# Gated cross-attention and ternary FFN on one core: plain V products for the second context too, an earlier read-out on ScalarE, and moved ternary steps

## The chip, the cores and the metric

The kernel runs on one core of a Trainium2 chip. Times are device microseconds (us) of that core. The kernel before took 1602.74 us, the median of 3 runs (1601.34 to 1603.58). Engines are named as in the profile: PE is TensorE's matmul, PEld its weight load, DVE is VectorE, ACT is ScalarE, POOL is GpSimd, SP is SyncE, which issues most DMAs.

## The reference

For 8 batches of 1024 rows and 512 channels, with g0 and g1 two gates:

```
q, k, v = layernorm(x) @ w_q, ctx @ w_k, ctx @ w_v
s       = (q @ k.T) / sqrt(512), causal mask
x       = x + tanh(g0) * (softmax(s) @ v)
h       = gelu(layernorm(x) @ ternary(W1).T + b1)        # W1: 2048 x 512
out     = x + tanh(g1) * (h @ ternary(W2).T + b2)        # W2: 512 x 2048
ternary(w) = clip(round(w / mean|w|), -1, 1)
```

All of it is computed near float32: an operand is held as a high and a low float16 half, and a product is three passes (`PASSES`: high·high, low·high, high·low). The ternary weights are exact in float16 and need two passes.

## The kernel before

**Two phases.** The attention runs over 64 slots. Slot t works on row tile t (128 rows); eight tiles (`TB`) share one batch, so tile i = t mod 8 of a batch sees i + 1 blocks of its context. Behind the slots the FFN runs over 16 groups of 4 tiles, in 64 units (`NU`).

**One slot on PE.** Scores of tile t (`s_ps`, 12 matmuls per 512 columns), the product that makes the query side of tile t + 2 (`t_product`, 24 matmuls of 256 columns), a part of the V projection of the next batch, then softmax times V of tile t - 1 (`o_ps`). The scores' width grows with i, so slots with i = 0 or 1 are short and those with i = 7 long. Scores of an even slot wait for `t_lower` (DVE) of the odd slot before it (`t_split`).

**V in two ways.** The first batch's V is made tile by tile: `v_product`, 12 matmuls of 512 columns each, read out by `v_upper` (ACT) and `v_lower` (DVE). From the second batch on a pair of tiles (256 rows) is a 2 x 2 block matrix, and a seven-product scheme makes it: products 1 to 7 of 6 matmuls of 256 columns (`v_part`). There are `NP` = 28 pairs. Pair u starts in slot 4 + 2u (`SPLIT_AT`: sums of the context's blocks on POOL, `ctx_parts`), has products 1 and 2 at the end of the odd slot 5 + 2u (`PRE_AT`, `v_pre`), products 6, 5, 7, 3 in the even slot 6 + 2u (`MAIN_AT`) and product 4 in slot 7 + 2u (`LAST_AT`). Products 1, 6, 5 and 3 share one PSUM bank `vp_a`; so product 6, the first thing that PE does in an even slot, waits until ACT has copied product 1 to `vr` (`v_first`, `vr_out`), and product 5 until ACT has copied product 6 (`v_second`, L737), which itself waits for `v21_lower` (DVE, L1104) of the pair before. The sums of weight blocks for it are split in `weight_parts_upper` (ACT, slot 4) and `weight_parts_lower` (DVE, slots 4 and 5, L1053).

**Order.** The program is written out by hand: each engine has a `slot` function that calls the pieces in its own order, and each engine runs them strictly in that order; semaphores join them. In an odd slot ACT does `softmax`, `t_upper` (L785), `rows_upper` (L793, which waits for DVE's `ln_rows`, L1133), and only then `v_first` (L730) and `v21_upper` (L761). DVE does mask and maximum (L1193, L1195), layernorm statistics, `p_split` (L1215), `t_lower` (L1156), `ln_rows`, the V read-outs, a ternary step where there is one, and then the update of `x_ring` with the attention's output (L1259), for which PE waits one tile later.

**Ternary weights.** 16 chunks of 1024 columns are made ternary by three DVE instructions each (`ternary`, L1393 to L1396), 12 of them in slots set by the "T" entries of `W_PLAN`, 4 in the first units of the FFN. **First FFN rows.** In slots 57 to 62 the first tiles' second layernorm is already made (`y_stats`, `y_normal`, and on POOL `y_scale`, `y_sums`, `y_lower`); `add_bias` (POOL, L640) adds b2 to the residual of the first four tiles in slots 61 and 62. `weight_sums` (DVE, L1298, slots 61 and 62) makes sums of W1 blocks.

## Time and profile before

| what | value |
|---|---|
| median of 3 runs | 1602.74 us |
| the profiled execution's own time | 1603.13 us |
| its span | 1601.3 us |
| PE busy | 1560.5 us (97%) |
| DVE busy | 1173.0 us (73%) |
| ACT busy | 881.7 us (55%) |
| POOL busy | 608.6 us (38%) |
| mean DMA rate | 107 GB/s |

A span is from the first to the last instruction; the time is the span and what lies around it, here 1.8 us. PE's busy time is read as time in which matmuls were in flight; it isn't work at full rate, since at the half clock the same matmul takes twice as long. The idle time of an engine counts only where the next engine in the chain waits for it.

### The profile page before, as it was taken

Reading aid. Unit: us, or ns where it says so; the run is one execution under the profiler, and the core shown is the slowest. Engines: PE = TensorE matmul, PEld = TensorE weight load, DVE = VectorE, ACT = ScalarE, POOL = GpSimd, SP = SyncE. Lnnn points to the kernel's source line nnn. Section 1 sums busy time; section 2 is a strip of 40 time slices with the busy share of each in tenths; the row PEclk is TensorE's granted clock in tenths of the full one; section 3 lists DMA queues with packets and bytes.
Section 4 is the critical chain, followed back from the end, with each engine's and each line's share of the span. In section 5 each row is a group of like instructions: output and inputs, shape, how many; then the busy total and the mean of one; then the engine's idle time right before and its main releaser. Section 6 shows DMA issues by size and latency. Waiting matters only on the chain.

```text
span 1601.3 us, 27829 instructions
## 1 busy us (share of the span) xinstructions
PE 1560.5 (97%) x10528; PEld 1028.5 (64%) x10528; DVE 1173.0 (73%) x1993; ACT 881.7 (55%) x1595; POOL 608.6 (38%) x585
## 2 busy tenths in 40 slices
PE   8889999999999999999999999999999999999998
PEld 4556666666666666665666666666666666666665
DVE  5767868788888888877776676767776677667654
ACT  4334545544444444344666666666666666666664
POOL 4323323332333323344353453444344443345320
PEclk9999999999999999999999999999999999999999
DMA  7536767756455545545523242223223333224110
GB/s 210 139 88 149 175 146 186 158 132 147 117 147 138 150 113 148 124 120 114 142 76 74 54 99 76 76 47 99 77 77 65 81 85 85 78 51 100 50 50 27
DMA packets 310997, 170.92 MB, mean 107 GB/s; under 512 B 268544, under 2 KB 268560, under 8 KB 310608
## 3 DMA queue, kind: packets, MB, share of 16 engines
q1 hardware_dynamic: 309392, 166.52, 43.1%
q10 hardware_dynamic: 1296, 2.36, 0.4%
q8 instruction: 83, 1.36, 0.3%
q14 instruction: 50, 0.41, 0.1%
q0 software_dynamic: 176, 0.27, 0.1%
HBM read 70.53 MB, written 33.55 MB: 65 GB/s over the span
## 4 chain that ended last, share of the span: by engine, by line
PE 74%; DVE 16%; issue 4%; ACT 4%; DMA 1%; SPq 0%; POOL 0%; DVEq 0%; ACTq 0%
PE s_ps L1556 13%; PE e_ps L1556 13%; PE s_ps L1692 7%; PE t_ps L1498 7%; PE o_ps L1498 7%; PE v_ps L1498 7%; PE o_ps L1739 6%; PE t_ps L1651 5%; PE e_ps L1594 4%; PE m_ps L1498 3%; DVE ctx_s L982 2%; DVE negmax L1195 1%; DVE x_ring L1259 1%; DVE xn_both L1133 1%; DVE v_work L1061 1%
## 5 line engine op out<-in xcount | busy, mean ns | idle before, releaser
L1350 DVE SCALAR_TENSOR_TENSOR v_s<-xnT,sc,v_s 128x512 f16<-128x512 f32 x256 | 238.6, 952 | 106.2 <-ACT v_s L909 106.2
L902 ACT ACTIVATE xnT<-tT,b_s 128x256 f32<-128x256 f32 x384 | 174.0, 500 | 179.7 <-DVE tT L1338 64.9
L1556 PE MATMUL s_ps<-raw,v_s 128*128 128x512 f16 x1024 | 263.0, 380 | 0.8 <-DVE raw L1396 0.8
L1556 PE MATMUL e_ps<-raw,v_s 128*128 128x512 f16 x1024 | 262.9, 379 | 0.0
L1692 PE MATMUL s_ps<-ctx_s,tT 128*128 128x512 f16 (+3 forms) x1152 | 202.0, 331 | 3.4 <-DVE tT L1156 2.6
L1739 PE MATMUL o_ps<-v_s,pT 128*128 128x512 f16 x840 | 193.2, 382 | 2.4 <-DVE x_ring L1259 2.4
L909 ACT ACTIVATE v_s<-xnT,sc 128x512 f16<-128x512 f32 x256 | 176.2, 712 | 7.5
L1556 PEld LDWEIGHTS e_ps<-raw,v_s 128*128 128x128 f16 x1024 | 100.2, 98 | 120.8
L646 POOL TENSOR_TENSOR tT<-tT 128x512 f32<-128x512 f32 x64 | 81.2, 1269 | 244.5 <-ACT tT L929 244.5
L1651 PE MATMUL t_ps<-xnT,a_s 128*128 128x256 f16 x1488 | 172.8, 273 | 0.1
L559 POOL TENSOR_TENSOR rstd<-var_s,minus_half 128x1 f32<-128x1 f32 x61 | 59.9, 983 | 291.8 <-DVE var_s L1127 291.8
L1692 PEld LDWEIGHTS s_ps<-ctx_s,tT 128*128 128x128 f16 x1152 | 107.1, 99 | 93.0 <-issue 6.2
L1651 PEld LDWEIGHTS t_ps<-xnT,a_s 128*128 128x128 f16 x1488 | 145.4, 98 | 20.9 <-DMA xnT<-xn_both 0.3
L1556 PEld LDWEIGHTS s_ps<-raw,v_s 128*128 128x128 f16 x1024 | 100.1, 98 | 68.1 <-issue 1.1
L1739 PEld LDWEIGHTS o_ps<-v_s,pT 128*128 128x128 f16 x840 | 82.5, 98 | 90.7 <-issue 4.9
L770 ACT ACTIVATE p<-s_ps,ebias,esc 128x128 f32<-128x128 f32 (+3 forms) x64 | 53.1, 830 | 154.3 <-DVE ebias L1199 154.0
L563 POOL TENSOR_TENSOR xn_both<-xn_both 128x512 f16<-128x512 f32 x61 | 70.5, 1156 | 151.3 <-ACT xn_both L793 151.3
L614 POOL TENSOR_TENSOR rstd<-var_s,minus_half 128x1 f32<-128x1 f32 x64 | 36.2, 565 | 221.8 <-DVE var_s L1310 221.8
L1332 DVE COPY tT<-t_ps 128x512 f32<-128x512 f32 x64 | 44.2, 691 | 85.0 <-PE t_ps L1498 85.0
L793 ACT ACTIVATE xn_both<-xn_both 128x512 f16<-128x512 f32 x64 | 40.3, 629 | 100.3 <-DVE xn_both L1133 100.3
L1594 PE MATMUL e_ps<-v_work 128*128 128x256 f16 x504 | 70.7, 278 | 20.7 <-ACT vr L730 16.3
L1344 DVE TENSOR_TENSOR tT<-tT,t_ps 128x512 f32<-128x512 f32 x64 | 44.0, 688 | 50.3 <-ACT tT L923 26.2
(229 smaller groups left out, 2882.7 us busy)
## 6 DMA issues: line engine op xcount, KB each, us to landing
out_y<-x_ring SPq DMA_DIRECT2D x128, 256.0 KB, 2.2
x_ring<-in_x SPq DMA_DIRECT2D x63, 256.0 KB, 2.9
raw<-in_ctxT SPq DMA_DIRECT2D x28, 512.0 KB, 3.8
v_work<-out_y SPq DMA_DIRECT2D x40, 256.0 KB, 3.8
w_in<-in_w1T SPq DMA_DIRECT2D x16, 512.0 KB, 3.9
w_in<-in_w2T SPq DMA_DIRECT2D x12, 512.0 KB, 4.0
x_ring<-out_y SPq DMA_DIRECT2D x22, 256.0 KB, 4.0
xnT<-xn_both SPq DMA_TRANSPOSE x128, 2.5
```

Of the source, the lines that this page charges most:

```text
L559: g.tensor_tensor(rstd[:, r:r + 1], var_s[:, r:r + 1], minus_half[:, :], ALU.pow).then_inc(ln_rstd, 1)
L563: g.tensor_tensor(xn_s[:, r, LO], xn32[:, r], xn_s[:, r, HI], ALU.subtract).then_inc(xn_lo, 1)
L646: g.tensor_tensor(rr[:, R3], rr[:, R3], rr[:, R5], ALU.add).then_inc(c22_sum, 1)
L902: a.activation(g32n[:, j, half * 2 * P:(half + 1) * 2 * P], src, ACT.Gelu, bias=b1_s[:, f:f + 1], scale=1.0 / YN).then_inc(g_act, 1)
L909: a.activation(g_s[:, U % 2, j, HI], g32n[:, j], ACT.Copy, scale=col(C_SG)).then_inc(g_hi, 1)
L1350: v.scalar_tensor_tensor(out=g_s[:, U % 2, j, LO], in0=g32n[:, j], scalar=col(C_SG), in1=g_s[:, U % 2, j, HI], op0=ALU.mult, op1=ALU.subtr ...
L1498: last_mm = mm(bank[:, p * 2 * P:(p + 1) * 2 * P], w, yT[g % 2][:, a, row, c, :], start=(first and p == 0 and a == HI and c == 0), stop=(a ...
L1556: last_mm = mm(y_ps[i], g_s[:, U % 2, j, a, i * P:(i + 1) * P], w2_s[:, f, :], start=(U % UG == 0 and n == 0 and a == HI), stop=(U % UG == ...
L1594: last_mm = mm(bank, left(ca, c), right(va, c), start=(first and n == 0 and c == 0), stop=(n == 2 and c == 1), skip_group_check=True)
L1651: last_mm = mm(bank[:, dd], a_s[:, aa, c, d * P:(d + 1) * P], xnT[:, pr, xa, c, :], start=(n == 0 and c == 0), stop=(n == 2 and c == DC - 1))
L1692: last_mm = mm(s_ps[:, lo:hi], tT[:, pr, ta, c, q * P:(q + 1) * P], ctx_s[:, par, ca, c, lo:hi], start=(n == 0 and c == 0), stop=(n == 2 a ...
L1739: last_mm = mm(o_bank(last, s), pT[:, (s - 1) % 2, pa, j], v_s[:, par, va, j], start=(n == 0 and j == 0), stop=(n == 2 and j == jn))
```

## The change

`PLAIN` = 2 batches now have their V made tile by tile. `v_product`, `v_upper` and `v_lower` run while t + 1 < 16 instead of t + 1 < 8, so 8 tiles move to the plain way and `NP` falls from 28 to 24 pairs; the four numbers `SPLIT_AT` to `LAST_AT` become 12 to 15. The second context is scaled and split in slots 5, 6 and 7 (`FIRST_SPLITS`), the third is loaded one slot behind each. Its maxima are taken in slots 8, 10 and 11. `weight_parts_lower` moves from slots 4 and 5 to 5 and 6. `v_first` moves on ACT ahead of `rows_upper`, for every pair but the first. The ternary steps of slots 31, 39 and 56 go to 32, 40 and 60; the buffers of the last ones change, and the waits for `x2_biased` and `w_ternary` with them. The four first `add_bias` go behind the slots, to POOL's start of the FFN.

```
-        NP = (NT - TB) // 2
-        SPLIT_AT, PRE_AT, MAIN_AT, LAST_AT = 4, 5, 6, 7
+        PLAIN = 2
+        NP = (NT - PLAIN * TB) // 2
+        SPLIT_AT, PRE_AT, MAIN_AT, LAST_AT = (TB * (PLAIN - 1) + n for n in (4, 5, 6, 7))
+        FIRST_SPLITS = {5: (0,), 6: (1, 2), 7: (3,)}
...
-                  **{t: "T" for t in (29, 30, 31, 37, 38, 39, 45, 46, 53, 54, 55, 56)}}
+                  **{t: "T" for t in (29, 30, 32, 37, 38, 40, 45, 46, 53, 54, 55, 60)}}
...
-                    sp.wait_ge(w_ternary, NW - W_LATE)
+                    sp.wait_ge(w_ternary, NW - W_LATE - 1)
...
+                for q in FIRST_SPLITS.get(t - 1, ()):
+                    load_ctx(2, q)
...
-                if last and e in (4, 5):
-                    add_bias(2 * e - 8)
-                    add_bias(2 * e - 7)
...
             last_sum(0)
             y_lower(2)
+            for e in range(GT):
+                add_bias(e)
...
                     t_upper(it, s)
+                if pre is not None and pre:
+                    v_first(pre)
                 if not last or t + LN_LEAD < NT:
                     rows_upper(it, s)
                 if t == 1:
                     ctx_upper(0, 0, 3)
+                for q in FIRST_SPLITS.get(t, ()):
+                    ctx_upper(1, 1, q)
                 if t == 4:
                     weight_parts_upper()
-                if t + 1 < TB:
+                if t + 1 < PLAIN * TB:
                     v_upper(it, s)
-                if pre is not None:
+                if pre == 0:
                     v_first(pre)
...
-                if t in (4, 5):
-                    weight_parts_lower(t - 4)
-                if t + 1 < TB:
+                if t in (5, 6):
+                    weight_parts_lower(t - 5)
+                if t + 1 < PLAIN * TB:
                     v_lower(it, s)
...
-                if n == NW - W_LATE:
-                    dve.wait_ge(x2_biased, 2)
...
-                v.tensor_scalar(w_neg[:, :], src, col(nth), None, ALU.is_lt).then_inc(w_negs, 1)
+                neg = w_neg[:, :]
+                if n == NW - W_LATE - 1:
+                    neg = w_in[:, (m + 1) % WR].bitcast(F16)[:, 0:WCH]
+                if n >= NW - W_LATE:
+                    neg = pT[:, 0, 0].rearrange("p j n -> p (j n)")
+                v.tensor_scalar(neg, src, col(nth), None, ALU.is_lt).then_inc(w_negs, 1)
...
-                if t + 1 < TB and t != PRE_AT:
+                if t + 1 < PLAIN * TB and t != PRE_AT:
                     v_product(it, s)
```

PE from the scores of slot 7 on, before: `t_ps` is the query product, the rows with `v_work` or a width of 256 in `e_ps` and `v_ps` are parts of the seven products, `o_ps` is softmax times V.

```order
L1692 MATMUL s_ps<-ctx_s,tT 128x512 x24
L1651 MATMUL t_ps<-xnT,a_s 128x256 x24
L1594 MATMUL e_ps<-v_work,ctx_s 128x256 x6
L1594 MATMUL e_ps<-wv_s,ctx_s 128x256 x6
L1594 MATMUL v_ps<-wv_s,ctx_s 128x256 x6
L1739 MATMUL o_ps<-v_s,pT 128x512 x21
L1594 MATMUL e_ps<-v_work 128x256 x6
L1692 MATMUL s_ps<-ctx_s,tT 128x128 x12
```

The same place now; L1682 is the plain product.

```order
L1704 MATMUL s_ps<-ctx_s,tT 128x512 x24
L1663 MATMUL t_ps<-xnT,a_s 128x256 x24
L1682 MATMUL v_ps<-wv_s,ctx_s 128x512 x12
L1751 MATMUL o_ps<-v_s,pT 128x512 x21
L1704 MATMUL s_ps<-ctx_s,tT 128x128 x12
```

All pieces of the seven products are gone from slots 5 to 13, and one plain product stands in each.

ACT in slot 33, an odd slot with i = 1, before: the first row is the exponential, then the high half of p, `t_upper`, `rows_upper` (L793), `v_first` (L730), `v21_upper` (L761) and, of the next slot, `v_second` (L737) and `v_third`.

```order
L770 ACTIVATE p,rowsum<-s_ps,ebias,esc 128x256
L775 ACTIVATE p_s<-p 128x256
L785 ACTIVATE tT<-t_ps 128x512
L793 ACTIVATE xn_both<-xn_both 128x512
L730 ACTIVATE vr<-e_ps 128x256
L761 ACTIVATE v_s<-vr 128x256
L737 ACTIVATE vr<-e_ps 128x256
L742 ACTIVATE vr<-e_ps 128x256
```

And now, with `v_first` as L733 and `rows_upper` as L796.

```order
L773 ACTIVATE p,rowsum<-s_ps,ebias,esc 128x256
L778 ACTIVATE p_s<-p 128x256
L788 ACTIVATE tT<-t_ps 128x512
L733 ACTIVATE vr<-e_ps 128x256
L796 ACTIVATE xn_both<-xn_both 128x512
L764 ACTIVATE v_s<-vr 128x256
L740 ACTIVATE vr<-e_ps 128x256
L745 ACTIVATE vr<-e_ps 128x256
```

Only the fourth and fifth row change places: `v_first` no longer stands behind an instruction that waits for DVE's `ln_rows`.

DVE in slot 60 from `t_lower` on, before: three V read-outs, the update of `x_ring` (L1252 to L1259), `y_normal` (L1324), and the mask of slot 61.

```order
L1156 SCALAR_TENSOR_TENSOR tT<-t_ps,tT 128x512
L1076 TENSOR_TENSOR vr<-vr,e_ps 128x256
L1088 SCALAR_TENSOR_TENSOR v_s<-e_ps,v_s 128x256
L1096 SCALAR_TENSOR_TENSOR v_s<-vr,v_s 128x2x256
L1252 RECIPROCAL rinv<-rowsum 128x1
L1255 TENSOR_SCALAR osc<-rinv,fsc 128x1
L1259 SCALAR_TENSOR_TENSOR x_ring<-o_ps,osc,x_ring 128x512
L1324 TENSOR_SCALAR v_s<-x_ring,mv,rstd 128x512
L1193 TENSOR_TENSOR s_ps<-s_ps,causal 128x128
```

And now.

```order
L1163 SCALAR_TENSOR_TENSOR tT<-t_ps,tT 128x512
L1083 TENSOR_TENSOR vr<-vr,e_ps 128x256
L1095 SCALAR_TENSOR_TENSOR v_s<-e_ps,v_s 128x256
L1103 SCALAR_TENSOR_TENSOR v_s<-vr,v_s 128x2x256
L1405 TENSOR_SCALAR w_in<-w_in,sc 128x1024
L1406 TENSOR_SCALAR raw<-w_in,sc 128x1024
L1408 TENSOR_TENSOR raw<-raw,w_in 128x1024
L1259 RECIPROCAL rinv<-rowsum 128x1
L1262 TENSOR_SCALAR osc<-rinv,fsc 128x1
L1266 SCALAR_TENSOR_TENSOR x_ring<-o_ps,osc,x_ring 128x512
L1333 TENSOR_SCALAR v_s<-x_ring,mv,rstd 128x512
L1200 TENSOR_TENSOR s_ps<-s_ps,causal 128x128
```

The ternary step that stood in slot 56 now stands ahead of the update of `x_ring` in slot 60.

## Rows read from the trace of the kernel before

**Rows 1.** The page: span, busy time of PE, the chain's shares by engine.
```profile
span 1601.3 us, 27829 instructions
...
PE 1560.5 (97%) x10528; PEld 1028.5 (64%) x10528; DVE 1173.0 (73%) x1993; ACT 881.7 (55%) x1595; POOL 608.6 (38%) x585
...
PE 74%; DVE 16%; issue 4%; ACT 4%; DMA 1%; SPq 0%; POOL 0%; DVEq 0%; ACTq 0%
```

**Rows 2.** Waits of PE, 60 to 770 us: us in total, times, longest.
```profile
PE e_ps L1594 <- ACT vr L730: 16.3, 13, 3.2
PE e_ps L1594 <- DVE v_work L1053: 4.3, 1, 4.3
PE o_ps L1739 <- DVE x_ring L1259: 2.4, 1, 2.4
```

**Rows 3.** Stretches: length, busy by engine (x instructions), then PE's clock, DMA.
```profile
102.71:109.54 6.83, 5.42 (x16) 2.34 (x17) 4.03 (x6) 0.38 (x1) 3.26 (x4) 0.50 0.34 86
423.57:426.98 3.41, 3.41 (x14) 1.79 (x13) 3.16 (x6) 0.44 (x2) 3.33 (x5) 0.50 0.32 92
```

**Rows 4.** Timeline of PE, slots 4 and 8: start, us, instruction, [idle before].
```profile
80.83 2.75 PE L1670 MATMUL v_ps<-wv_s,ctx_s 128*128 128x512 f16 x12
83.42 0.38 PE L1739 MATMUL o_ps<-v_s,pT 128*128 128x512 f16 x1
...
141.92 0.82 PE L1594 MATMUL e_ps<-v_work 128*128 128x256 f16 x6
142.58 0.82 PE L1594 MATMUL e_ps<-wv_s,v_work 128*128 128x256 f16 x6
```

**Rows 5.** Timeline of DVE and PE where slot 6 begins.
```profile
102.18 1.79 DVE L1053 SCALAR_TENSOR_TENSOR v_work<-v_s,sc,v_work 128x1024 f16<-128x1024 f32 x1
...
104.12 1.44 PE L1594 MATMUL e_ps<-v_work 128*128 128x256 f16 x6 [4.29 <-DVE v_work L1053]
```

**Rows 6.** Timeline of DVE, ACT and PE at the end of slot 9.
```profile
154.01 0.69 DVE L1156 SCALAR_TENSOR_TENSOR tT<-t_ps,tT 128x512 f16<-128x512 f32 x1
155.18 0.63 ACT L793 ACTIVATE xn_both<-xn_both 128x512 f16<-128x512 f32 x1 [2.00 <-DVE xn_both L1133]
155.72 0.36 ACT L730 ACTIVATE vr<-e_ps 128x256 f32<-128x256 f32 x1
156.14 0.83 PE L1594 MATMUL e_ps<-v_work 128*128 128x256 f16 x6 [1.02 <-ACT vr L730]
156.52 0.81 DVE L1104 SCALAR_TENSOR_TENSOR v_s<-vr,v_s 128x256 f16<-128x256 f32 x1
```

**Rows 7.** Timeline of PE where slots 34 and 58 begin.
```profile
423.38 1.31 PE L1594 MATMUL e_ps<-v_work 128*128 128x256 f16 x6 [2.24 <-ACT vr L730]
...
693.31 1.46 PE L1594 MATMUL e_ps<-v_work 128*128 128x256 f16 x6 [3.18 <-ACT vr L730]
```

**Rows 8.** The ternary lines in the slots: ns min/median/max; one POOL bias add.
```profile
L1393 DVE TENSOR_SCALAR g<-w_in,sc x12: 740/1209/1271, 377.0 to 682.4; 128x1024 f16<-128x1024 f32 x12
L1394 DVE TENSOR_SCALAR w_s<-w_in,sc x8: 740/1210/1214, 378.2 to 571.7; 128x1024 f16<-128x1024 f32 x8
L1396 DVE TENSOR_TENSOR w_s<-w_s,g x8: 693/1095/1098, 379.4 to 572.5; 128x1024 f16<-128x1024 f16 x8
740.96 1.26 POOL L640 TENSOR_TENSOR v_work<-g,b_row 128x512 f32<-128x512 f32 x1
```

**Rows 9.** Timeline, slots 56 to 61: PE's scores of 57, then DVE.
```profile
683.42 1.47 PE L1692 MATMUL s_ps<-ctx_s,tT 128*128 128x256 f16 x12
684.87 0.75 DVE L1259 SCALAR_TENSOR_TENSOR x_ring<-o_ps,osc,x_ring 128x512 f32<-128x512 f32 x1
693.36 0.42 DVE L1070 TENSOR_TENSOR vr<-vr,v_ps 128x256 f32<-128x256 f32 x1 [0.71 <-ACT vr L730]
697.74 0.30 DVE L1193 TENSOR_TENSOR s_ps<-s_ps,causal 128x128 f32<-128x128 f32 x1 [1.17 <-PE s_ps L1692]
740.24 0.75 DVE L1259 SCALAR_TENSOR_TENSOR x_ring<-o_ps,osc,x_ring 128x512 f32<-128x512 f32 x1
```

More of the change, by code:

```diff
@@ L237, in pair_at @@
         def pair_at(u):
-            b, q = 1 + u // NQ, u % NQ
+            b, q = PLAIN + u // NQ, u % NQ
             return b, q, b % 2
@@ L247, in gated_block @@
         B12_DONE, BD_DONE, B21_DONE = 1, 2, 3
-        MAX_AT = {2: (1, (0, 1)), 3: (1, (2, 3))}
-        for b in range(2, B):
+        MAX_AT = {2: (1, (0, 1)), 3: (1, (2, 3)), 8: (2, (0, 1)), 10: (2, (2,)), 11: (2, (3,))}
+        for b in range(PLAIN + 1, B):
             for q, at in enumerate((-3, -1, 1, 3)):
@@ L268, in gated_block @@
         W_CHUNKS = [(src, dst, k) for src, dst in ((w1T, w1_s), (w2T, w2_s)) for k in range(DC * FC * P // WCH)]
-        W_FIRST = NQ * 6
+        W_FIRST = NQ * (B - 1 - PLAIN)
         NW = len(W_CHUNKS)
@@ L365, in load_ctx @@
                 sp.wait_ge(ctx_split, NQ * (batch - 1) + q + 1)
-                if batch >= 2:
-                    sp.wait_ge(sums_made, 4 * (NQ * (batch - 2) + q + 1))
+                if batch > PLAIN:
+                    sp.wait_ge(sums_made, 4 * (NQ * (batch - 1 - PLAIN) + q + 1))
                 sp.dma_start(raw_q[:, q], ctx_batches[batch][:, q]).then_inc(ctx_in[q], 16)
@@ L451, in slot @@
                 if u is not None and u + NQ < NP:
-                    load_ctx(2 + u // NQ, u % NQ)
+                    load_ctx(PLAIN + 1 + u // NQ, u % NQ)
                 if last and t == NT - 8:
@@ L1262, in slot @@
                     ctx_lower(0, 0, 3)
+                for q in FIRST_SPLITS.get(t, ()):
+                    ctx_lower(1, 1, q)
                 if t in MAX_AT:
@@ L1598, in v_pre @@
             def v_pre(u):
-                pe.wait_ge(ctx_split, NQ + u + 1)
+                pe.wait_ge(ctx_split, NQ * PLAIN + u + 1)
                 if u:
@@ L1604, in v_pre @@
                 if u == 1:
-                    pe.wait_ge(v_split, TB)
+                    pe.wait_ge(v_split, PLAIN * TB)
                 if u:
@@ L1725, in slot @@
                     pe.wait_ge(p_turned[(s - 1) % 2], p_turned_by(it, s - 1))
-                    if t <= TB:
+                    if t <= PLAIN * TB:
                         pe.wait_ge(v_split, t)
                     else:
-                        u = (t - 1 - TB) // 2
+                        u = (t - 1 - PLAIN * TB) // 2
                         pe.wait_ge(vb_split, nth_of(u, B12_DONE))
```

2 lines of the change are left out of this document (1 added, 1 removed).

## The prediction, made before the changed kernel had run

> **What bounds the kernel now.** I read the page first: PE is busy for 1560.5 of 1601.3 us, and the chain that ended last lies on PE for 74% and on DVE for 16% [rows 1]. So a microsecond is won only where PE does less, stops standing, or stops running at half clock. The second view is PE's waits over the slots [rows 2]: three groups matter. Thirteen times product 6 of a pair waits for ScalarE's read-out of product 1 (16.3 us in total); once it waits for DVE's weight sums (4.3); once the product with V waits for DVE's update of `x_ring` (2.4). The third view is the granted clock by stretch [rows 3]: behind the wait of 4.3 us PE runs 6.83 us at 0.50, its lower level of 1.2 GHz, and behind the wait of 2.24 us in slot 33 it does so for 3.41 us. Work done at that level would have taken half the time at 2.4 GHz, so the first stretch costs 5.42 / 2 = 2.7 us and the second 3.41 / 2 = 1.7. The timelines then say what the waiting instruction really waited for. The FFN behind the slots is PE without a gap to speak of, and the change leaves its products as they are.
>
> **Plain instead of seven products (slots 5 to 15).** A plain product starts at 80.83 and the next work at 83.42, so it is 2.59 us of PE; six matmuls of 256 columns go from 141.92 to 142.58, 0.66 us [rows 4]. A pair costs 7 x 0.66 = 4.6 us in seven products and 2 x 2.59 = 5.2 plain, so four pairs add 4 x 0.6 = +2.4 us. This is work on PE, and nothing hides it.
>
> A rule in the Trainium skill would have it otherwise (TensorE: Matmul & The Clock Gate, "Back-to-back issue gap"): it gives 131 ns per matmul of 512 columns in a sustained stream and 81 ns at 128. By it a plain product would be 12 x 131 ns = 1.6 us and, with 106 ns between the two for 256 columns as an estimate, the pair would save about 1.3 us, 5 us for four. By that rule the sum would come out 7 us lower. The trace does not agree: it has 216 ns for each of these very matmuls [rows 4]. The measurement decides, and I give the rule no chance.
>
> What it takes away: product 6 in slot 6 waited 4.29 us for the second `weight_parts_lower`, which ended at 103.97 because it stands in DVE's queue behind a wait for `v_first` [rows 5]. Now these sums are made in slots 5 and 6 and first used in slot 14, eight slots later, so wait and half clock go: -4.3 - 2.7 = -7.0 us. What is late next in slot 13, where the first pair's product 1 is read out in the old place? There ScalarE's queue holds `rows_upper` and `v_upper` ahead, as in slot 5; but DVE comes to the mask without the weight sums of 1.3 to 1.8 us and without their wait for ScalarE, and PE has a product with V of 15 matmuls (15 x 0.216 = 3.2 us) before it asks. I take no wait, and keep up to 1.5 us in the range. In the plain slots DVE has one read-out of a bank per slot instead of six smaller instructions and the low half of the sums per pair, so it gets lighter; the scaling of the second context comes to slots 5 to 7, which are long on PE (i = 5 to 7). The third context's four loads are issued by SP at the end of slots 6 to 8 and used by DVE at the end of slots 8 to 11, a slot or more later; what stands behind them on SP are the transposes of rows used two slots later. I take 0 for both.
>
> **`v_first` ahead of `rows_upper`.** In slot 9 [rows 6] ScalarE stood 2.00 us for DVE's `ln_rows`, then did `rows_upper` (0.63) and only at 155.72 the read-out, which PE had been waiting for since 155.12 (156.14 - 1.02). Product 1 ends before product 2 and the product with V, so in the new place the read-out falls into those 2.00 us: it costs ScalarE nothing, and it is done before PE is. What is late next? Product 6 then starts at 155.12 and the scores of slot 10 at 155.78; they need `t_lower`, which ended at 154.70: 1.1 us to spare. Product 5 comes 12 x 0.162 = 1.9 us later (384 columns), at 157.7; it needs the read-out of product 6, which stands behind `v21_lower`, ended at 157.33 before and some 0.4 us earlier now, because ScalarE no longer has 0.36 us of `v_first` ahead of `v21_upper`. So 157.0 + 0.4 = 157.4: just in time. In slots with i = 3 the scores are wider and there is more room. The thirteen waits are those of the slots with i = 1 and 3, two of which fall into slots 9 and 11, where now there are no seven products at all. I take twelve of them whole: 16.3 - 3.2 (slot 57, below) = -13.1 us. In slot 33 the wait was 2.24 us and was followed by half clock [rows 3, 7]: a further -1.7 us.
>
> **Ternary steps.** A step is 3.5 us where POOL works beside it and 2.1 us where it doesn't (medians 1.21 + 1.21 + 1.10, least 0.74 + 0.74 + 0.69 [rows 8]). POOL makes the context's block sums at the start of even slots, which is when DVE gets to the step of slot 31 or 39; in slots 32 and 40 the step comes when POOL has only the norm, and just ahead of an update of `x_ring` that waits for PE anyway. So DVE comes to slots 33 and 41 no later than now, rather about a microsecond earlier, and this is what lets me take the 2.24 us whole.
>
> The Trainium skill (SBUF — State Buffer, "SBUF: two separate sides") says that DVE in a two-port mode and GpSimd take one shared pair of ports as an exclusive lock. The trace has both prices for the same instruction, 0.74 and 1.21 us, so it agrees as far as it goes; if slot 60's step met such work after all, the sum would be 1.4 us higher.
>
> Slot 57 is different. Its wait of 3.18 us [rows 7] with the half clock behind it (1.7) ought to be worth 4.9 us, and PE does come to slot 58 that much earlier. But from there DVE is the engine that is behind: from the update at 684.87 to the one at 740.24 [rows 9] it rarely stands, and PE waits for the last one (2.4 us [rows 2]). So this stretch is worth what DVE's path becomes. Without the step in slot 56 the update can start about where the product that it reads ends and PE's next scores start, 683.42; with 0.3 us for the end of that product, 683.7: -1.2. The wait for `v_first` goes: -0.7. The wait for PE's scores goes, since PE is early: -1.2. The step now in slot 60, with POOL at rest: +2.1. Sum -1.0 us instead of -4.9. PE's wait in slot 61 becomes longer, about 3.5 to 4 us, partly moved to the scores of slot 62; the half clock behind it may grow by up to 1 us.
>
> **First residual sums.** Four adds of 1.26 us each [rows 8] leave POOL in slots 61 and 62, where they ran beside `y_normal` and beside the last p split on DVE; this may give some tenths at the last product with V. In the FFN they stand behind `y_lower` and ahead of `y_scale` of a group that isn't urgent; their sums are asked for only when the first group is finished, some units later. I take 0, at worst 4 x 1.26 = 5 us of delay for `y_scale` and, with the first units full of PE work, none of it on the path.
>
> **Sum.** +2.4 - 7.0 - 13.1 - 1.7 - 1.0 = -20.4 us against the profiled execution's 1603.13, so 1582.7. That execution was 0.4 us above the median shown, so against the median 1582.3; I say 1582.
>
> **Rivals.**
> 1. *The waits of product 6 come back at the next place*: at the scores (`t_lower`) or at product 5 (`v_second`), because DVE, which had a rest of 0.7 us in each of these waits, is now driven faster than it can go in the short slots. For it: only some 0.3 us to spare at product 5 by my own working. Against: scores had 1.1 us to spare. Ten waits remain outside slots 9, 11 and 57, 11.3 us (13.1 less 1.9); half of it back is +5.7, all but the clock +8: 1588 to 1590.
> 2. *Slot 57's gain is kept*: -4.9 instead of -1.0, and no longer half clock: 1578. Against it is the row of the wait at slot 61; for it, that DVE's waits inside the stretch (for ACT and for POOL's `y_lower`) may shrink too.
> 3. *Slower*: `v_first` now holds ScalarE's queue until PE has finished product 1, and behind it stand `rows_upper`, POOL's low half, SP's transposes and the query product. The place is every odd slot from 15 on, 23 of them. If rows then came late, each would cost PE what ScalarE is late; it decides from 20.4 / 23 = 0.9 us a slot; at 1 us it costs 23. Against: product 1 is done before `ln_rows` in rows 6, and the rows are used two slots later. It would give 1582.7 + 23 = 1606.
> 4. *The change doesn't do what it says in slots 4 to 15*: a wait in slot 13 or in the plain slots like the 4.29 us, with its clock loss: +7, 1589.
>
> **Chances.** Forecast 0.68 (its own range 1580 to 1585), rival 1 0.12, rival 2 0.10, rival 3 0.03, rival 4 0.07. The unknowns within the forecast (1.5 us in slot 13, 1.4 us for the step in slot 60, 1 us of clock, some tenths at the end) and the runs' spread of 2.2 us give 1580 to 1586; to leave out no more than 2 in 10 I take in rival 2 and most of rivals 1 and 4, 1577 to 1589. A change under 0.2% (3.2 us) can't be told from none: faster 0.95, same 0.02, slower 0.03.
>
> **What would show it.** Right: no row of PE waiting for the read-out of product 1 but perhaps in slot 13; no granted clock of 0.50 near 103 and near 424; the plain products in slots 4 to 14 at 2.59 us without gaps; seven-product matmuls down from 1176 to 1008; a longer wait of PE for `x_ring` in slot 61, at a time about 20 us earlier than 741; the FFN as long as before. Wrong: waits of PE for `t_lower` or the second read-out of a microsecond each in slots with i = 1, or PE's wait in slot 61 gone.

## The result, and the profile after

The changed kernel takes 1586.12 us (median of 4 runs, 1584.63 to 1586.78), the kernel before, run beside it, 1603.16 (1601.34 to 1604.01). The ratio is 0.9894, with a 95% interval of 0.9877 to 0.9911: 17.0 us faster. 20.4 us and 1582 were forecast, so the change gives a sixth less than that; the time lies inside the range given (1577 to 1589), but outside the forecast's own (1580 to 1585).

The page of the changed kernel, which answers to [rows 1]: the span, the busy times, the chain.

```profile
span 1582.8 us, 27584 instructions
...
PE 1554.9 (98%) x10456; PEld 1019.6 (64%) x10456; DVE 1165.2 (74%) x1973; ACT 871.8 (55%) x1575; POOL 590.3 (37%) x569
...
PE 72%; DVE 16%; ACT 5%; issue 4%; DMA 1%; POOL 0%; SPq 0%; DVEq 0%; ACTq 0%
```

PE is still the bound. It is busy for only 5.6 us less than before, while the span fell by 18.5: most of the gain is time in which PE stood. PE's waits over 60 to 790 us say which standing went, and what came (beside [rows 2]; the line numbers are those of the changed kernel, L1606 a seven-product matmul, L740 the read-out of product 6, `v_second`, L1266 the update of `x_ring`, L1163 `t_lower`, L1341 the FFN's first copy on DVE):

```profile
PE e_ps L1606 <- ACT vr L740: 4.0, 6, 1.3
PE o_ps L1751 <- DVE x_ring L1266: 3.5, 1, 3.5
PE s_ps L1704 <- DVE tT L1163: 1.9, 3, 0.7
PE t_ps L1510 <- DVE tT L1341: 1.4, 1, 1.4
PE e_ps L1751 <- DMA pT<-p_s: 0.4, 1, 0.4
```

No row is left of PE waiting for product 1's read-out (16.3 us before) or for the weight sums (4.3). Two rows are new: six waits for the *other* read-out, 4.0 us, and one of 1.4 us at the start of the FFN. Granted clock by stretch, against [rows 3] (the third column from the end is PE's clock):

```profile
32.63:36.05 3.42, 3.42 (x18) 2.43 (x17) 3.35 (x5) 2.04 (x2) 2.26 (x1) 0.50 0.01 2
101.00:108.00 7.00, 7.00 (x48) 4.43 (x46) 4.75 (x11) 2.65 (x5) 0.55 (x1) 1.00 0.39 95
412.00:419.00 7.00, 6.82 (x55) 5.11 (x53) 6.41 (x15) 2.74 (x7) 3.70 (x6) 1.00 0.55 135
722.13:725.54 3.41, 3.41 (x10) 1.20 (x9) 2.30 (x6) 1.91 (x3) 0.55 (x1) 0.50 1.00 213
```

Near 103 us and in slots 33 and 34 PE now has 2.4 GHz, and the stretch of half clock that followed the wait of 3.18 us in slot 57 is gone too; behind the wait of 3.5 us it still falls to 1.2 GHz, as it did before. The first row is worth a look, because it isn't the change's doing: of the kernel before the same place reads

```profile
31.03:37.86 6.83, 4.84 (x23) 3.46 (x24) 6.52 (x14) 2.38 (x4) 3.89 (x2) 0.50 0.20 49
```

The start is the same program in both. Of the profiled executions of this study some had the short stretch there and some the long one (the experiments e7 and f2, for instance, the long one). The profiled execution of the changed kernel is its fastest run of four and has the short one. Slot 5's scores, which start 1.2 us earlier in it than in the kernel before, lie between 84.0 and 85.2 us in the seven profiled executions with the short stretch and between 85.4 and 86.7 in the seven with the long one. So spans are compared from a fixed instruction behind the start, slot 4's scores, and whole times by their medians.

The span by stretch, from PE's rows of both kernels at the same places: scores of slots 5, 16 and 57, and the FFN's first product with W2. Before:

```profile
86.01 4.06 PE L1692 MATMUL s_ps<-ctx_s,tT 128*128 128x512 f16 x24
226.64 0.83 PE L1692 MATMUL s_ps<-ctx_s,tT 128*128 128x128 f16 x12
...
771.29 1.03 PE L1556 MATMUL s_ps<-raw,v_s 128*128 128x512 f16 x4
```

After:

```profile
84.80 4.06 PE L1704 MATMUL s_ps<-ctx_s,tT 128*128 128x512 f16 x24
218.27 0.83 PE L1704 MATMUL s_ps<-ctx_s,tT 128*128 128x128 f16 x12
...
664.87 1.47 PE L1704 MATMUL s_ps<-ctx_s,tT 128*128 128x256 f16 x12
...
751.47 1.03 PE L1568 MATMUL s_ps<-raw,v_s 128*128 128x512 f16 x4
```

With 683.42 of [rows 9] for slot 57 before, the lengths are:

| stretch | before | after | difference | forecast |
|---|---|---|---|---|
| start to slot 5 | 86.01 | 84.80 | -1.2 | 0 |
| slots 5 to 16 (plain V) | 140.63 | 133.47 | -7.2 | +2.4 - 7.0 - 1.9 = -6.5 |
| slots 16 to 57 | 456.78 | 446.60 | -10.2 | -11.2 - 1.7 = -12.9 |
| slot 57 to the FFN's first product | 87.87 | 86.60 | -1.3 | -1.0 |
| the rest | 830.01 | 831.33 | +1.3 | 0 |
| span | 1601.3 | 1582.8 | -18.5 | -20.4 |

Without the 1.2 us at the start, it is 17.3, about what the medians say. Set against the forecast that leaves some 3 us missing, in two places: slots 16 to 57 (2.7), and the start of the FFN (1.3); slots 5 to 16 and the end of the slots gave 1.0 more.

### The profile page after: what moved, and what is told of

Read it like the earlier page. It is cut to its first block, busy times and chain, and to the rows that moved or that the text cites. A ratio compares the mean times of both kernels' runs of the same rounds, so it can differ in the third digit from the quotient of the medians.

```text
span 1582.8 us, 27584 instructions
## 1 busy us (share of the span) xinstructions
PE 1554.9 (98%) x10456; PEld 1019.6 (64%) x10456; DVE 1165.2 (74%) x1973; ACT 871.8 (55%) x1575; POOL 590.3 (37%) x569
## 4 chain that ended last, share of the span: by engine, by line
PE 72%; DVE 16%; ACT 5%; issue 4%; DMA 1%; POOL 0%; SPq 0%; DVEq 0%; ACTq 0%
PE s_ps L1568 14%; PE e_ps L1568 13%; PE t_ps L1510 7%; PE v_ps L1510 7%; PE o_ps L1510 7%; PE o_ps L1751 6%; PE s_ps L1704 5%; PE t_ps L1663 5%; PE m_ps L1510 3%; PE e_ps L1606 2%; PE v_ps L1682 2%; DVE negmax L1202 2%; DVE ctx_s L989 2%; DVE x_ring L1266 1%; DVE xn_both L1140 1%
## 5 line engine op out<-in xcount | busy, mean ns | idle before, releaser
L1359 DVE SCALAR_TENSOR_TENSOR v_s<-xnT,sc,v_s 128x512 f16<-128x512 f32 x256 | 239.5, 956 | 105.7 <-ACT v_s L916 105.7
L1704 PE MATMUL s_ps<-ctx_s,tT 128*128 128x512 f16 (+3 forms) x1152 | 197.7, 326 | 4.7 <-DVE tT L1163 3.9
L563 POOL TENSOR_TENSOR rstd<-var_s,minus_half 128x1 f32<-128x1 f32 x61 | 56.0, 919 | 291.7 <-DVE var_s L1134 291.7
L615 POOL TENSOR_TENSOR rstd<-var_s,minus_half 128x1 f32<-128x1 f32 x64 | 36.1, 565 | 218.8 <-DVE var_s L1319 218.8
L1341 DVE COPY tT<-t_ps 128x512 f32<-128x512 f32 x64 | 44.2, 691 | 85.0 <-PE t_ps L1510 85.0
L796 ACT ACTIVATE xn_both<-xn_both 128x512 f16<-128x512 f32 x64 | 40.3, 630 | 90.5 <-DVE xn_both L1140 90.0
L641 POOL TENSOR_TENSOR v_work<-v_work,b_row 128x512 f32<-128x512 f32 x40 | 75.4, 1913 | 0.0
```

Source lines behind the costliest of these rows:

```text
L563: g.tensor_tensor(rstd[:, r:r + 1], var_s[:, r:r + 1], minus_half[:, :], ALU.pow).then_inc(ln_rstd, 1)
L641: g.tensor_tensor(x2, x2_first(e), b2_row[:, :], ALU.add).then_inc(x2_biased, 1)
L1359: v.scalar_tensor_tensor(out=g_s[:, U % 2, j, LO], in0=g32n[:, j], scalar=col(C_SG), in1=g_s[:, U % 2, j, HI], op0=ALU.mult, op1=ALU.subtr ...
L1704: last_mm = mm(s_ps[:, lo:hi], tT[:, pr, ta, c, q * P:(q + 1) * P], ctx_s[:, par, ca, c, lo:hi], start=(n == 0 and c == 0), stop=(n == 2 a ...
```

## The experiments

Each time stands beside the kernel before on the same chip; "gain" is the difference of these medians, and the changed kernel's is 17.0. A gain's interval is 2 to 3 us to each side, so smaller differences between two experiments are read from their traces. "From slot 4 on" is the time from the start of slot 4's scores to the end of the profiled execution; a table behind the last experiment has it for every run.

### One part at a time: the read-out, the plain context

e1 undoes only the place of `v_first` in the changed kernel:

```
-                if pre is not None and pre:
-                    v_first(pre)
                 if not last or t + LN_LEAD < NT:
                     rows_upper(it, s)
...
-                if pre == 0:
+                if pre is not None:
                     v_first(pre)
```

> The changed kernel (1586.1 us) with one thing undone: the read-out of product 1 stands behind rows_upper again in every odd slot. My theory (the read-out's place is worth the waits of product 6 in slots 15 to 55): the waits for that read-out come back in the slots with i = 1 and 3, ten or eleven of 0.7 to 1.3 us and the one of slot 57, 11 to 13 us in sum less what DVE gives back at the 3.5 us wait in slot 61; the time is 1595 to 1598. Rival A (the steps moved to slots 32 and 40 and not the read-out's place took the waits away): no more than 3 us, 1587 to 1589. Rival B (the waits only hid DVE's lag, and come out elsewhere): the waits for product 1 come back but those for the second read-out and x_ring go, 1590 to 1592.

Measured: 1591.32 us against 1602.95, ratio 0.9936 (0.9923 to 0.9949), gain 11.6. My number (1595 to 1598) was wrong. Rival B had the time, and half of the account: the waits for the second read-out go, as it says, but that for `x_ring` stays at 3.5 us. PE's waits of e1:

```profile
PE e_ps L1604 <- ACT vr L733: 11.4, 11, 2.0
PE o_ps L1749 <- DVE x_ring L1264: 3.5, 1, 3.5
...
PE s_ps L1702 <- DVE tT L1161: 1.3, 2, 0.7
```

The eleven waits come back whole, 11.4 us, just as counted. But the 4.0 us for the second read-out are gone in exchange, and 0.6 of `t_lower`'s: 11.4 - 4.0 - 0.6 = 6.8, and the two spans, with the same short stretch at the start, are 1589.5 and 1582.8. So the new place removes 11.4 us of waits and earns 6.7 by the traces, 5.4 by the medians.

e2 makes the same move alone, in the kernel before:

```
+                if pre is not None and pre:
+                    v_first(pre)
                 if not last or t + LN_LEAD < NT:
                     rows_upper(it, s)
```

> The kernel before (1603.2 us) with one thing done: the read-out of product 1 ahead of rows_upper for every pair but the first. If the parts add up as in my sum, all thirteen waits of product 6 go but those that a ternary step in slots 31, 39 and 56 causes: 9 to 11 us, the time 1592 to 1594; the wait of 4.3 us near 104 us and its half clock stay. If the new place pays only together with the moved steps, slots 32 and 33, 40 and 41 and 57 still wait, and the waits for t_lower or the second read-out take over elsewhere: 1597 to 1600.

Measured: 1591.28 us against 1602.95, ratio 0.9931 (0.9917 to 0.9945), gain 11.7, a little beyond the first case. The row of its waits for ScalarE:

```profile
PE e_ps L1596 <- ACT vr L737: 5.5, 6, 1.3
```

All thirteen waits for product 1 go, even in slots 33, 41 and 57 with the ternary steps in their old slots, and 5.5 us come for the second read-out. Alone it takes off 11.7; all the rest of the change without it (e1) takes off 11.6; together 17.0 (from slot 4 on 11.0, 10.7 and 17.3). The two don't add up, because both lift the same waits: of the 16.3 us the plain context and the moved steps remove 4.9 anyway, and three of the four stretches of half clock between slot 4 and the end (e1's one stands at 680 us, in slot 58, behind a wait of 2.02 us).

e3 puts the second context back to seven products:

```
-        PLAIN = 2
+        PLAIN = 1
...
-                if t in (5, 6):
-                    weight_parts_lower(t - 5)
+                if t in (4, 5):
+                    weight_parts_lower(t - 4)
```

> The changed kernel with the plain V taken back to the first context alone (28 pairs in seven products, the weight sums in slots 4 and 5, the maxima and splits of the second context as before); the read-out's place, the ternary steps and the residual sums stay as changed. My theory (plain costs 2.4 us and takes away a wait of 4.3 us and 2.7 us of half clock, near 104 us): 1586.1 + 7.0 - 2.4 = 1590.7, between 1589.5 and 1592. Rival A (the second plain context is what saves, waits of its four pairs included): 1593 or more. Rival B (what DVE is late in slot 6 has gone with the read-out's place and steps): no wait near 104, 1583.7.

Measured: 1590.96 us against 1602.95, ratio 0.9929 (0.9916 to 0.9942), gain 12.0: 5.0 less than the changed kernel, where 4.6 was worked out. The wait is back, and with it half clock until 110.5:

```profile
104.82 1.44 PE L1606 MATMUL e_ps<-v_work 128*128 128x256 f16 x6 [4.29 <-DVE v_work L1060]
```

From slot 5's scores to slot 16's e3 takes 138.65 us (86.72 to 225.37), the changed kernel 133.47: 5.2 us.

### The ternary steps

e5 moves two steps back, e6 the last one:

```
-(29, 30, 32, 37, 38, 40, 45, 46, 53, 54, 55, 60)
+(29, 30, 31, 37, 38, 39, 45, 46, 53, 54, 55, 60)      # e5
+(29, 30, 32, 37, 38, 40, 45, 46, 53, 54, 55, 56)      # e6
```

> The changed kernel with two ternary steps back in slots 31 and 39 (from 32 and 40). Theory (with the step ahead of it DVE is late for the mask and the ln_rows of the next slots, and the step costs 3.5 us beside POOL's block sums instead of 2.1): PE waits 1 to 2 us more in slots 32 to 33 and 40 to 41, once perhaps with 1.7 us of half clock behind it: 1588 to 1591. Rival (with the read-out early, slot 33 no longer waits for DVE, so the steps' place is worth nothing): 1585.5 to 1586.5; it could even be shorter, since the waits for the second read-out in slots 32 and 40 (1.3 and 0.7 us) would find DVE at another phase.

Measured: 1586.51 us against 1602.06, ratio 0.9905 (0.989 to 0.992), gain 15.6. My 1588 to 1591 was too high. 1.4 us of 17.0 is less than the intervals can part, but the trace shows where it lies, two slots on and at product 5, not where I looked for it:

```profile
413.31 0.83 PE L1606 MATMUL e_ps<-v_work 128*128 128x256 f16 x6 [0.98 <-ACT vr L740]
501.89 0.83 PE L1606 MATMUL e_ps<-v_work 128*128 128x256 f16 x6 [0.98 <-ACT vr L740]
```

Both waits are 0.18 in the changed kernel. From product 5 of slot 32 to that of slot 34 e5 takes 20.42 us (392.89 to 413.31), the changed kernel 19.27 (393.73 to 413.00): the place of a step is worth 1.15 us, 0.8 of it in this wait, the rest in pauses under 0.2 us. For both that is 2.3 us in the trace and 1.4 in the medians. The step itself takes 3.5 us in slots 31 and 39 of e5 and 2.1 in slots 32 and 40 of the changed kernel, as I had it.

> The changed kernel with the last early ternary step back in slot 56 (from 60). Theory (DVE's path from the update in slot 56 to the last one bounds this stretch): a step of 3.5 us in slot 56 instead of 2.1 us in slot 60, so PE comes to the last product with V 1.2 to 1.5 us later: 1587.3 to 1587.8, and PE waits earlier, in slot 57 or 58, instead of 3.5 us in slot 61. Rival A (PE's waits have gone with the read-out's place, and where the step stands is no matter): 1586. Rival B: the wait in slot 57 is long enough for half clock: 1589.

Measured: 1585.4 us against 1602.06, ratio 0.9895 (0.988 to 0.991), gain 16.7: no difference. The price was wrong: DVE's rows of e6 in slot 56, and its next long wait,

```profile
664.85 0.74 DVE L1405 TENSOR_SCALAR w_in<-w_in,sc 128x1024 f16<-128x1024 f32 x1
665.51 0.74 DVE L1406 TENSOR_SCALAR raw<-w_in,sc 128x1024 f16<-128x1024 f32 x1
666.29 0.69 DVE L1408 TENSOR_TENSOR raw<-raw,w_in 128x1024 f16<-128x1024 f16 x1
...
700.08 0.55 DVE L1333 TENSOR_SCALAR v_s<-x_ring,mv,rstd 128x512 f32<-128x512 f32 x1 [3.79 <-POOL v_s L632]
```

show 2.1 us, as in slot 60, not the 3.5 us beside POOL that I took; it was so in the kernel before too, where the first of them, the last of [rows 8]'s range at 682.4, took 0.74 us. Wherever the step stands, PE waits 5.7 to 5.8 us in slots 56 to 62, only elsewhere: this is DVE's path. And that path holds a wait of 3.79 us for POOL's first `y_lower` (L632).

### What the second read-out waits for

e7 gives product 6's read-out two buffers, so that it doesn't wait for `v21_lower` of the pair before:

```
-        vr = sb("vr", [P, 3, D // 2])
+        vr = sb("vr", [P, 4, D // 2])
...
-                if u:
-                    act.wait_ge(vb_split, nth_of(u - 1, B21_DONE))
-                a.activation(vr[:, 2], vp_a, ACT.Copy).then_inc(vr_out, 1)
+                if u >= 2:
+                    act.wait_ge(vb_split, nth_of(u - 2, B21_DONE))
+                a.activation(vr[:, 2 + u % 2], vp_a, ACT.Copy).then_inc(vr_out, 1)
```

> The changed kernel with two buffers for the read-out of product 6, so that it needn't wait for v21_lower of the pair before. Theory (the six waits for the second read-out, 4.0 us, come from that wait alone; they are the price of my rival 1 in slots with i = 0): they go, and nothing else is late in those slots, 1582 to 1583. Rival (DVE is late as a whole there, and PE waits a moment later for t_lower or the V sums instead): half or less comes out, 1584.5 to 1586.

Measured: 1583.58 us against 1602.06, ratio 0.9882 (0.9866 to 0.9899), gain 18.5, between my two cases; the span is 1581.1, with slot 4's scores at 73.74 (73.09 in the changed kernel), so 2.35 us less from there on. Of the 4.0 us 0.2 are left, and 1.5 come elsewhere, each under 0.6: `t_lower` 0.8 more, product 1's read-out 0.5, a context split 0.2. So the theory holds for the waits that it names, and more than a third of them comes back a moment later, as the rival has it.

Why slots 32, 40 and 48, and not 16 and 24? Rows of the changed kernel at slot 24 and at slot 32 (DVE's `v21_lower`, then PE's product 6; in slot 32 also POOL, the scores, ScalarE's read-out and product 5):

```profile
302.86 1.18 DVE L1111 SCALAR_TENSOR_TENSOR v_s<-vr,v_s 128x256 f16<-128x256 f32 x1 [0.35 <-ACT v_s L764]
304.23 0.82 PE L1606 MATMUL e_ps<-v_work 128*128 128x256 f16 x6
...
390.90 0.82 PE L1606 MATMUL e_ps<-v_work 128*128 128x256 f16 x6
391.56 0.83 PE L1704 MATMUL s_ps<-ctx_s,tT 128*128 128x128 f16 x12
391.76 1.16 POOL L567 TENSOR_TENSOR xn_both<-xn_both 128x512 f16<-128x512 f32 x1 [2.87 <-ACT xn_both L796]
392.02 1.18 DVE L1111 SCALAR_TENSOR_TENSOR v_s<-vr,v_s 128x256 f16<-128x256 f32 x1 [0.34 <-ACT v_s L764]
393.29 0.38 ACT L740 ACTIVATE vr<-e_ps 128x256 f32<-128x256 f32 x1 [1.30 <-DVE v_s L1111]
393.73 0.83 PE L1606 MATMUL e_ps<-v_work 128*128 128x256 f16 x6 [1.34 <-ACT vr L740]
```

In slot 24 `v21_lower` starts 1.4 us ahead of product 6, in slot 32 1.1 us behind it, with two ternary steps on DVE in slots 29 and 30. That these steps make it late is argued and not shown, for no run moves them; and they can't be all of it, since slot 56 has steps in slots 53 to 55 before it, and there `v21_lower` still starts 0.7 us ahead (653.07 and 653.78) and PE doesn't wait. And in a slot with i = 0 the scores between products 6 and 5 are 12 matmuls of 128 columns, 391.56 to 392.39: 0.8 us of cover, where slot 10, on which the forecast was worked, had 1.9.

### The start of the FFN

e4 puts the four residual sums back into slots 61 and 62, e8 puts them behind unit 0:

```
+                if last and e in (4, 5):          # e4
+                    add_bias(2 * e - 8)
+                    add_bias(2 * e - 7)
...
+                if U == 0:                        # e8
+                    for e in range(GT):
+                        add_bias(e)
```

> The changed kernel with the first four residual sums back in slots 61 and 62. Theory (they delay DVE at the start of the FFN, as the new wait of 1.4 us at 768.65 says): that wait goes, y_normal in slot 61 and the last p split are slower again by 0.5 to 1 us; the time is between 1 us shorter and the same, 1585 to 1586. Rival A: the adds in slots 61 and 62 cost DVE as much on the path as they give at the start of the FFN, or more: 1586.5 to 1588.

Measured: 1584.87 us against 1602.95, ratio 0.9891 (0.9877 to 0.9905), gain 18.1.

> The changed kernel with the first four residual sums made by POOL at the end of the FFN's unit 0 instead of ahead of it. Theory (they hold the shared port while DVE makes y_stats and y_normal of slot 62 and the late ternary steps, and that is the new wait of 1.4 us at 768.65): that wait goes, 1584.5 to 1585. Rival A: the contention only moves to the late steps of units 0 and 1, and the wait there (0.8 us) grows by as much: 1586. Rival B: the wait of 1.4 us comes from the late ternary step being late for its load: unchanged, 1586.

Measured: 1586.49 us against 1602.06, ratio 0.9901 (0.9886 to 0.9915), gain 15.6. The changed kernel's rows at the start of the FFN (POOL's adds, DVE beside them, PE's wait):

```profile
749.18 1.71 POOL L641 TENSOR_TENSOR v_work<-ctx_s,b_row 128x512 f32<-128x512 f32 x1
...
752.08 2.94 POOL L641 TENSOR_TENSOR v_work<-x_ring,b_row 128x512 f32<-128x512 f32 x2
752.54 3.03 DVE L1359 SCALAR_TENSOR_TENSOR v_s<-xnT,sc,v_s 128x512 f16<-128x512 f32 x2
...
768.65 1.05 PE L1510 MATMUL t_ps<-ctx_s,a_s 128*128 128x256 f16 x8 [1.38 <-DVE tT L1341]
```

The two splits of L1359 take 3.03 us beside the adds; in e4 nothing runs beside them:

```profile
753.36 1.41 DVE L1360 SCALAR_TENSOR_TENSOR v_s<-xnT,sc,v_s 128x512 f16<-128x512 f32 x2
```

In e4 PE's wait of 1.38 us is gone, and 0.4 us more are waited for the last p's transpose: 0.9 us less from slot 4 on (73.51 to 1582.3 against 73.09 to 1582.8). The medians differ by 1.1, which the intervals don't part. In e8 the one wait becomes two, of 1.04 and 1.23 us, the second for ScalarE: moving the adds further back doesn't help. That the residual sums cost 1.4 us at the FFN's start is shown by the traces; that the whole kernel gains by their return is 0.9 us of one pair of traces, and the medians don't settle it.

### What bounds slots 57 to 62

f1 moves the weight sums of slot 61 behind the update for which PE waits; f2 makes the third `y_normal`, which waits 3.79 us for POOL, a slot later:

```
-                if last and t == NT - 3:            # f1: ahead of the update
-                    weight_sums(0)
-                    weight_sums(1)
+                if last and t == NT - 2:            # behind y_stats, slot 62
+                    weight_sums(1)
+                if last and t == NT - 3:            # end of slot 61
+                    weight_sums(0)
...
-                if y_row is not None:               # f2
+                if y_row == 3:
+                    y_normal(2)
+                if y_row is not None and y_row != 2:
                     y_normal(y_row)
```

> The changed kernel with the two weight sums of slot 61 (5.8 us of DVE ahead of the update that PE waits 3.5 us for) put behind that update: the first at the end of slot 61, the second in slot 62 behind y_stats. Theory (those sums are what PE waits for, and nothing else is late there): the wait of 3.5 us and the half clock behind it (1.7) go, 1581 to 1582. Rival (DVE is behind as a whole since the product with POOL's y_lower; what leaves this place is late at the mask of slot 62 or at the FFN's first products): 1584 or more, with a new wait for DVE after 715.

Measured: 1581.62 us against 1602.09, ratio 0.9873 (0.9858 to 0.9888), gain 20.5. The wait of 3.51 us and its half clock are gone, and the rival has a part: a new wait of 1.69 us for the exponential of slot 62.

```profile
723.75 5.34 PE L1705 MATMUL s_ps<-ctx_s,tT 128*128 128x512 f16 x24 [1.69 <-ACT p L773]
```

3.51 + 1.71 (half of 3.41) - 1.69 = 3.5 us; the spans differ by 3.3.

> The changed kernel with the third y_normal made at the end of slot 60 instead of slot 59, where DVE stands 3.8 us for POOL's first y_lower. Theory (DVE's path over slots 57 to 61 holds this standing time, so it, and not the place of the ternary step, sets when PE goes on): the waits of slots 60 and 62 for t_lower (0.66, 0.63) go and the wait of 3.5 us shrinks by 2 to 3 us, perhaps with the half clock: 1581.5 to 1584. Rival (DVE would have waited for PE or ScalarE there anyway, as the step in slot 56 or 60 made no difference): 1586.

Measured: 1582.36 us against 1602.09, ratio 0.988 (0.9863 to 0.9896), gain 19.7: the theory. The wait is 2.39 us instead of 3.51, no half clock follows it (1.7), and slot 62's wait for `t_lower` (0.63) is gone: 3.5 us, and 3.3 in the spans from slot 4 on (its own is at 74.07). That the half clock went because the wait got shorter isn't shown: the kernel before lost it behind a wait of the same 2.39 us at 741.13. So 1.7 us of f2's gain hang on something that these runs don't part.

```profile
720.99 4.04 PE L1753 MATMUL o_ps<-v_s,pT 128*128 128x512 f16 x18 [2.39 <-DVE x_ring L1266]
```

Why are the weight sums so long? DVE's and POOL's rows of the changed kernel (the row of 716.35 is the second instruction of the pair at 715.75):

```profile
714.54 1.29 DVE L1307 TENSOR_TENSOR wv_s<-w_s 128x1024 f16<-128x1024 f16 x2
715.75 4.67 DVE L1307 TENSOR_TENSOR wv_s<-wv_s,w_s 128x1024 f16<-128x1024 f16 x2
715.83 4.03 POOL L632 TENSOR_TENSOR v_s<-v_s 128x1792 f16<-128x1792 f32 x1 [3.99 <-ACT v_s L860]
716.35 4.07 DVE L1307 TENSOR_TENSOR wv_s<-wv_s,w_s 128x1024 f16<-128x1024 f16 x1
```

A pair takes 1.29 us alone. The second instruction of the next pair is issued while POOL's subtraction runs, and ends 0.56 us behind that subtraction's end (719.86): it stood for all of it, then did its own half microsecond. The subtraction takes 3.58 us at 694.18, where no such pair runs; its 0.45 us more here are about what was left of DVE's first instruction when it started. The Trainium skill says this ("SBUF — State Buffer", section "SBUF: two separate sides"): the side that starts first has the shared pair of ports for its whole instruction, and the other fully blocks. The trace agrees, with 4.07 us for an instruction of about 0.65. DVE and POOL stood so in the kernel before too (L1298, 4.67 us for the same pair at 735.21).

### All together

f3 joins e7, e4, f1 and f2. g1 takes f3 and moves two things again: both weight sums stand behind `y_stats` in slot 62, and of the residual sums only those of the first two tiles stay in slot 61, the others go behind POOL's last `y_lower`.

> The changed kernel with four edits together: two buffers for the read-out of product 6, the first residual sums in slots 61 and 62, the weight sums of slot 61 behind the update, the third y_normal in slot 60. If they add up: -3 (buffers), -1 (residual sums), -5.2 (sums) and up to -1.3 (t_lower in slots 60 and 62): 1575.5 to 1577. If PE, now earlier, runs into ScalarE's or DVE's work at the start of the FFN (1.4 us, or more): 1578 to 1580. If DVE is the bound of the last slots as a whole, it is 1581 to 1583, no better than two buffers and residual sums alone.

Measured: 1580.15 us against 1602.09, ratio 0.9863 (0.9848 to 0.9877), gain 21.9: just beyond the second case. Alone the four gains over the changed kernel's 17.0 were 1.5, 1.1, 3.5 and 2.7, together 8.8; 4.9 came. From slot 4 on it is 2.35, 0.9, 3.3 and 3.3, together 9.9, and 6.1 came. Most of the missing 3.8 us was never there twice: f1 takes away the wait of 3.51 us in slot 61 with its half clock, and f2's gain is 1.1 us of the same wait and the same 1.7 us, so 2.8 us stand in both. Some 0.7 us more are waited for the last p's transpose (1.59 us, 0.86 in e4). These two waits are left, the first as in f1 alone; DVE's and PE's rows of f3:

```profile
713.64 5.75 DVE L1311 TENSOR_TENSOR wv_s<-w_s 128x1024 f16<-128x1024 f16 x2
...
722.35 5.34 PE L1708 MATMUL s_ps<-ctx_s,tT 128*128 128x512 f16 x24 [1.64 <-ACT p L774]
...
732.45 2.35 DVE L1225 SCALAR_TENSOR_TENSOR p_s<-p,p_s 128x1024 f16<-128x1024 f32 x1 [1.85 <-ACT p_s L779]
...
739.51 0.82 PE L1755 MATMUL e_ps<-v_s,pT 128*128 128x512 f16 x3 [1.59 <-DMA pT<-p_s]
```

Both waits stand behind DVE instructions that ran beside POOL (5.75 us for a pair of 1.29, 2.35 for a split of 1.23). g1 moves them apart:

```
+                if last and t == NT - 2:
+                    weight_sums(0)
+                    weight_sums(1)
...
+                if last and e == 4:
+                    add_bias(0)
+                    add_bias(1)
...
+            for e in (2, 3):                        # behind y_lower(2)
+                add_bias(e)
```

> The kernel with four edits (1580.2 us) with two places changed again: both weight sums of slot 61 go to slot 62 behind y_stats (there the first took 5.75 us beside POOL at the end of slot 61, and PE waited 1.64 us for the exponential of slot 62), and only the residual sums of the first two tiles stay in slot 61, those of the next two go behind POOL's last y_lower (they ran beside the last p split, 2.35 instead of 1.23 us, and PE waited 1.59 us for its transpose). Theory: both waits come from those two pairs running side by side, so PE's wait for the exponential goes, and that for the transpose is 0.4 us again: 1577 to 1578. Rival: the waits come from PE being early as such, and DVE's or ScalarE's path behind them is no shorter: 1579.5 to 1580.5.

Measured: 1577.51 us (1577.3 to 1577.79, 5 runs) against 1602.49, ratio 0.9842 (0.9829 to 0.9856), gain 25.0. It beats both kernels, the changed one by 8.0 us. Its longest waits over 60 to 770 us:

```profile
PE s_ps L1709 <- DVE tT L1166: 2.1, 5, 0.8
PE v_ps L1515 <- ACT tT L933: 0.6, 1, 0.6
PE e_ps L1756 <- DMA pT<-p_s: 0.6, 1, 0.6
PE e_ps L1611 <- ACT vr L736: 0.5, 1, 0.5
```

One of 0.8 us for a late ternary step follows at 786 us, as it does in both kernels. The waits for the exponential of slot 62 and for the transpose are gone or short, as the theory has it. No stretch of half clock is left between the start and the end.

The gains over the kernel before, in us:

| run | by the medians | from slot 4 on |
|---|---|---|
| changed kernel | 17.0 | 17.3 |
| e1, read-out back | 11.6 | 10.7 |
| e2, read-out alone | 11.7 | 11.0 |
| e3, one plain context | 12.0 | 12.3 |
| e4, residual sums back | 18.1 | 18.2 |
| e5, two steps back | 15.6 | 14.8 |
| e6, last step back | 16.7 | 17.1 |
| e7, two buffers | 18.5 | 19.6 |
| e8, residual sums later | 15.6 | 16.2 |
| f1, weight sums behind | 20.5 | 20.6 |
| f2, third `y_normal` later | 19.7 | 20.6 |
| f3, four together | 21.9 | 23.4 |
| g1, moved again | 25.0 | 25.8 |

## Why the prediction was right, and where it fell short

**Plain V (+2.4 - 7.0): right.** Measured over slots 5 to 16 -7.2 instead of -6.5, with the two waits of slots 9 and 11; e3 gives 5.0 instead of 4.6 by itself (5.2 in its trace), so the plain products cost about 0.5 us less than I took. The matmuls of seven products are 1008 instead of 1176, the plain ones 192 instead of 96, both as forecast. Rival 4 (a wait in slot 13 or among the plain slots) did not come.

**`v_first` ahead (-13.1 - 1.7): the mechanism right, the size not.** All its waits went. The step that failed is "Product 5 comes 12 x 0.162 = 1.9 us later (384 columns), at 157.7" and what follows to "just in time". It was worked on slot 10, i = 2, and carried over to all others by "In slots with i = 3 the scores are wider and there is more room"; the even slots with i = 0 and only 0.8 us of scores were not worked out. In three of them (32, 40, 48) the second read-out takes the first one's place, 2.7 us in all; in slots with i = 2, with the cover of 1.9 us, it takes 0.18 us twice (34, 42) and 0.98 in slot 58, where DVE was late by more. That is 4.0 us in six waits, 3.0 of them in slots 16 to 57, where 2.7 us are missing. This is rival 1's mechanism, for which I had 5.7 to 8 us (all ten waits back would even be 11.3, not 8). I gave it 0.12 as an alternative to the forecast; it was a part that came with it, and its sign, waits for the second read-out, did show, in even slots and mostly under a microsecond. e7 shows the cause: it takes away what that read-out waits for, and 3.8 of the 4.0 us go, of which 1.5 come back elsewhere.

**Ternary steps.** Slot 33's 2.24 us could be taken whole, but not for the reason given: e2 has the steps in their old slots and no wait there either. With the steps moved and the read-out in its old place (e1) 1.07 us of it is left. So the read-out's place alone takes it all, and the rest of the change alone takes half of it. Once the read-out is early, what their move earns is 1.4 to 2.3 us at slots 34 and 42 (e5), mostly at product 5.

**Slots 57 to 61 (-1.0): right number, wrong account.** Up to the product for which PE waits it was -0.9 (664.87 to 721.67 against 683.42 [rows 9] to 741.13). That DVE's path bounds the stretch held, so rival 2 fell. The terms, between DVE's updates of `x_ring`: the first starts 1.2 us earlier against slot 57's scores (0.28 behind them instead of 1.45), as worked out. `v_first`'s 0.7 us did not come: it is 9.98 us to the next update instead of 9.99, since `v21_lower` now waits 0.34 us for ScalarE and takes 1.17 instead of 0.80. The stretch with the wait for PE's scores got 1.6 us shorter, not 1.2, and the step in slot 60 cost 2.0. That the sum still comes to -0.9 is luck in part: one term fell out, and others made up for it. The move of the step as such, -1.2 and +2.1 in my terms, is worth nothing (e6: it costs 2.1 us in either slot). And I did not see that the longest wait on the path is DVE's standing 3.79 us for `y_lower`, nor that the weight sums take 5.9 us for 2.6 us of work, though both stood in the trace before (719.24 and 734.00). Either of them was worth more than the terms I argued over (f2: 2.7, f1: 3.5 by the medians).

**Residual sums (0): wrong by 1.3 at the FFN's start.** I looked at POOL's queue, and it was free; I didn't ask whom the adds would slow on DVE where they went, though I had the two prices of [rows 8]. DVE's splits at the FFN's start went from 1.41 to 3.03 us, and PE waited 1.38 us sixteen us later. "The FFN as long as before" failed with it.

**Rival 3** (`v_first` holding ScalarE's queue) left no trace: over 60 to 790 us no row of PE waiting for layernorm's rows or their transposes.

## What to carry to other kernels

When a wait is taken away, work out the next condition in the *tightest* slot of the pattern, not in the one at hand: here a wait for one read-out of a bank hid the wait for the next, and an edit worth 11.7 us alone, beside others worth 11.6 without it, gave 17.0 with them. Nor do the gains of two edits add that shorten the same wait, as f1 and f2 do. And when work moves on one of two engines that share a port, look at both ends of the move for long instructions of the other: an instruction of 0.65 us stood 3.5 us for one of POOL, and taking such pairs apart, one more buffer and a later `y_normal`, with no less work, gave another 8.0 us.
